# Causal attention and the feed-forward's input, moved tile by tile into the loop of the second cross attention

## The chip, the cores and the metric

The kernel runs on one core of one Trainium2 chip. The metric is the time of one execution on the device, in microseconds (us); of several runs the median is given. The core has five engines with instruction queues of their own: TensorE (PE: matrix products and transposes; its weight loads are shown as PEld), VectorE (DVE), ScalarE (ACT), GpSimd (POOL) and SyncE (SP, which here only issues DMAs). Each works through its own queue in program order and waits on semaphores.

## The reference

Two layers work on latents x of 16 x 64 rows by 256 columns, with a context of 16 x 1024 rows. All is 32-bit float, 16 heads of 16.

```
x = x + L0_cross(norm(x), ctx, mask)      x = x + L1_cross(norm(x), ctx)
x = x + L0_linear_attention(norm(x))      x = x + L1_attn(norm(x))
x = x + L0_ffn_int8(norm(x))              x = x + L1_ffn_fp4(norm(x))

L1_attn:  Q, K, V = per-head 16x16 maps of x;  a = softmax(causal(Q K' / 4));  out = a V
          cat = heads side by side (b, s, 256);  scrambled = cat.transpose(0,2,1).reshape(b, s, 256)
          return scrambled @ W_O
L1_ffn:   fp4(x): per block of 16 columns, scale = max|x|/6, round x/scale to a 4-bit grid, times scale
          h = silu(fp4(x) @ fp4(w_gate)') * (fp4(x) @ fp4(w_up)')       (704 columns)
          return fp4(h) @ fp4(w_down)'
```

The cross attention reads all 64 latents of a batch and all 1024 context rows. Causal attention works inside one batch, and the feed-forward on each row alone.

## The kernel before, in words

The latents lie in SBUF as `lat`, 8 tiles of 128 rows (two batches each). The program is a row of blocks; each block frees its semaphores and ends at a barrier of all engines. This text is about the last two, `second_cross` (L1_cross) and `last_tiles` (L1_attn and L1_ffn). PSUM is 8 banks of 128 x 512 floats.

`second_cross` runs 64 steps, 4 for each of 16 batches, two heads times two halves of the work in each. Step s of TensorE is: `scores(s)` into banks 0 to 3, in even steps `times_v` for an earlier pair of steps, `project_v(s+2)`, `transposes(s-1, 0)`, in steps whose batch s//4+1 isn't in `EarlyKeys.BATCHES` `project_k(s+4)`, then `transposes(s-1, 1)`; every eighth step (s = 10, 18, ...) ends with `output`, after which tile (s-10)/8 of `lat` is complete. `scores(s)` waits for both exponentials of step s-1. All results but the scores rotate through banks 4 to 7 (`Banks.open`), so an open waits until the result four opens earlier has been taken. VectorE takes the two maxima (L859), the values (L841), half of the transposed probabilities (L869) and, once both exponentials are done, the inverses of the two row sums in one instruction (`inverses`, L892). GpSimd multiplies the two probabilities of 128 x 1024 by them (`normalise`, L655). ScalarE computes the exponentials (L802) and takes keys (L772) and the other half of the transposed probabilities (L813). Among these steps the weights of the fp4 feed-forward are quantised (`Fp4Weights`): for each of three matrices x eight VectorE steps from step `FW_STEPS[x]` on, one a step, a GpSimd step, and three groups of transposes. The seventh of the eight, `scalar_tensor_tensor` of 128 x 1536, is L180. Lines 173 to 181 (`fp4_steps`) serve the weights, the feed-forward's input and its hidden layer.

After the 64 steps, three more drain the last two pairs. `last_tiles` then runs causal attention and the feed-forward over the 8 tiles in 12 rounds: in round r causal scores of tile r, the rest of causal attention of tile r-1, its output and the feed-forward's input of tile r-2, gate and up of tile r-3, the hidden layer's rounding, transposes and down projection of tile r-4. Its own norms take 4 tiles at once (`Norm`, `sn`) or one (`fn`). It has buffers of its own (two of `prob` and `hid`, three of `value`), and all 8 banks rotate.

Names and lines for the steps below. Causal, on TensorE: L1911 transposes of the normed latents, L1924 queries and keys, L1929 values, L1943 scores, L1955 transposes of the probabilities, L1971 heads, L1983 transposes back, L1994 output. On VectorE: L2075 and L2080 logits and maxima, L2086 and L2090 division, L2095 output. On GpSimd: L2057 `spread_queries`, L2064 `distances`. Feed-forward: L2126 transposes of its input, L2136 gate and up, L2147 transposes of the hidden layer, L2158 down; L2226 product with up on VectorE, L2176 SiLU and L2183 to L2187 hidden copies on ScalarE, L2258 the last scaling on GpSimd, L2262 output. Norms: L1839 to L1868, of which L1849 is the square root on ScalarE. SiLU, Exp and Sqrt each need their table loaded on ScalarE; a copy doesn't.

## Time and profile before

| | |
|---|---|
| time before, median of 3 runs | 1401.79 us (1398.05 to 1402.02) |
| the profiled execution: time, span | 1398.16 us, 1396.3 us |
| PE busy in the span | 1279.3 us (92%) |
| DVE, ACT, POOL busy | 930.5 (67%), 784.7 (56%), 689.2 us (49%) |
| scores of step 0 and of step 63 of `second_cross` start | 729.14 and 1167.27 us |
| first instruction of `last_tiles` | 1184.24 us |
| mean clock granted to TensorE | 0.969 of full |

The span runs from the first to the last instruction of the execution; the time is 1.9 us longer. Times are us from the span's start unless ns is said. A busy TensorE is not one at its peak, since its instructions overlap: where work is back to back, the start of the next group minus the start of this one is what a group costs. In the rows, "[0.59 <-DVE ca_v L841]" means 0.59 us of idle time in front of the row, ended by that instruction of VectorE.

### The profile page before, as it was taken

Reading aid. Unit: us, or ns where it says so; the run is one execution under the profiler, and the core shown is the slowest. Engines: PE = TensorE matmul, PEld = TensorE weight load, DVE = VectorE, ACT = ScalarE, POOL = GpSimd, SP = SyncE. Lnnn points to the kernel's source line nnn. Section 1 sums busy time; section 2 is a strip of 40 time slices with the busy share of each in tenths; the row PEclk is TensorE's granted clock in tenths of the full one; section 3 lists DMA queues with packets and bytes.
Section 4 is the critical chain, followed back from the end, with each engine's and each line's share of the span. In section 5 each row is a group of like instructions: output and inputs, shape, how many; then the busy total and the mean of one; then the engine's idle time right before and its main releaser. Section 6 shows DMA issues by size and latency. Waiting matters only on the chain. (4 is left out here: it accounts for less than half of the span.)

```text
span 1396.3 us, 28298 instructions
## 1 busy us (share of the span) xinstructions
PE 1279.3 (92%) x11120; PEld 890.4 (64%) x11122; DVE 930.5 (67%) x1728; ACT 784.7 (56%) x1350; POOL 689.2 (49%) x383
## 2 busy tenths in 40 slices
PE   6999999999999999887879999999999997778876
PEld 3667666676676675555546677667667765655653
DVE  4685686765665654765857686777677766568774
ACT  3766656666666654554646666665666564344431
POOL 2755655566665652320036574665557665323311
PEclk9999999999999999999999999999999999688998
DMA  4322112111123002004521021031022300000000
GB/s 159 93 70 66 48 46 67 46 47 47 58 81 103 13 16 99 1 1 135 170 66 62 31 62 52 31 92 52 32 61 63 92 1 13 16 2 5 9 8 12
DMA packets 30530, 74.21 MB, mean 53 GB/s; under 512 B 4032, under 2 KB 16192, under 8 KB 26176
## 3 DMA queue, kind: packets, MB, share of 16 engines
q1 hardware_dynamic: 30400, 72.41, 16.9%
q8 instruction: 90, 1.47, 0.4%
q14 instruction: 40, 0.33, 0.1%
HBM read 65.06 MB, written 7.34 MB: 52 GB/s over the span
## 5 line engine op out<-in xcount | busy, mean ns | idle before, releaser
L655 POOL TENSOR_TENSOR ca_prob<-ca_prob,ca_inv_sum 128x1024 f32<-128x1024 f32 x256 | 493.2, 1948 | 345.8 <-DVE ca_inv_sum L892 345.8
L732 PEld LDWEIGHTS bank<-ident,ca_prob 128*128 128x128 f32 x2048 | 236.6, 141 | 85.1 <-issue 57.8
L732 PE MATMUL bank<-ident,ca_prob 128*128 128x128 f32 x2048 | 265.3, 274 | 13.7 <-POOL ca_prob L655 7.8
L856 DVE CUSTOM_DVE_ANT_0 ca_neg_logit<-bank,ca_mask_add 128x1024 f32<-128x1024 f32 x128 | 151.6, 1221 | 112.5 <-PE bank L722 81.4
L859 DVE TENSOR_REDUCE ca_neg_max<-bank 128x1 f32<-128x1024 f32 x128 | 150.6, 1218 | 79.1 <-PE bank L722 79.1
L802 ACT ACTIVATE ca_prob<-bank,ca_neg_max 128x1024 f32<-128x1024 f32 x128 | 142.7, 1115 | 88.5 <-DVE ca_neg_max L859 88.5
L802 ACT ACTIVATE ca_prob<-ca_neg_logit,ca_neg_max 128x1024 f32<-128x1024 f32 x128 | 146.8, 1149 | 72.8 <-DVE ca_neg_max L856 72.7
L869 DVE COPY ca_probT<-bank 128x512 f32<-128x512 f32 x256 | 163.5, 680 | 2.1 <-PE bank L732 2.1
L813 ACT ACTIVATE ca_probT<-bank 128x512 f32<-128x512 f32 x256 | 139.1, 595 | 24.8 <-PE bank L732 22.1
L722 PE MATMUL bank<-ca_kT,ca_q_blk 32*128 32x512 f32 x1024 | 146.0, 639 | 4.6 <-DVE ca_v L841 2.7
L772 ACT ACTIVATE ca_kT<-bank,ca_bk 64x512 f32<-64x512 f32 x128 | 87.4, 683 | 104.4 <-PE bank L667 103.5
L749 PEld LDWEIGHTS bank<-ca_probT,ca_v 128*32 128x32 f32 x4096 | 109.0, 110 | 48.1 <-issue 31.2
L667 PE MATMUL bank<-ca_ctxT,ca_wk 128*128 128x512 f32 x256 | 122.5, 603 | 11.7 <-DMA ca_bk<-in_L_xattn_bk 9.2
L749 PE MATMUL bank<-ca_probT,ca_v 128*32 128x128 f32 x4096 | 126.3, 276 | 1.4 <-ACT ca_probT L813 1.4
L681 PE MATMUL bank<-wv,ctxT 128*128 128x256 f32 x512 | 127.2, 392 | 0.0
L681 PE MATMUL bank<-ca_wv,ca_ctxT 128*128 128x256 f32 x512 | 127.2, 392 | 0.0
L681 PEld LDWEIGHTS bank<-wv,ctxT 128*128 128x128 f32 x512 | 92.2, 189 | 41.2 <-issue 31.3
L681 PEld LDWEIGHTS bank<-ca_wv,ca_ctxT 128*128 128x128 f32 x512 | 92.2, 189 | 41.2 <-issue 28.2
L772 ACT ACTIVATE ca_kT<-bank,ek_bk 64x512 f32<-64x512 f32 x80 | 54.6, 683 | 66.2 <-PE bank L667 65.6
L667 PE MATMUL bank<-ctxT,ek_wk 128*128 128x512 f32 x160 | 74.9, 593 | 2.1 <-PEq L100 2.1
L667 PEld LDWEIGHTS bank<-ca_ctxT,ca_wk 128*128 128x128 f32 x256 | 44.7, 194 | 45.8 <-issue 35.7
L841 DVE TENSOR_TENSOR ca_v<-bank,bv 128x512 f32<-128x512 f32 x64 | 43.8, 685 | 26.4 <-PE bank L681 26.4
(278 smaller groups left out, 1648.4 us busy)
## 6 DMA issues: line engine op xcount, KB each, us to landing
ca_ctxT<-in_ctxT SPq DMA_DIRECT2D x16, 1024.0 KB, 5.2
ctxT<-in_ctxT SPq DMA_DIRECT2D x16, 1024.0 KB, 4.9
ca_mask_i<-in_mask SPq DMA_DIRECT2D x32, 256.0 KB, 4.5
ek_ctxT<-in_ctxT SPq DMA_DIRECT2D x12, 512.0 KB, 5.5
early_k<-ek_out SPq DMA_DIRECT2D x48, 128.0 KB, 3.5
ca_kT<-early_k SPq DMA_DIRECT2D x12, 512.0 KB, 5.7
lat<-in_x SPq DMA_DIRECT2D x1, 1024.0 KB, 4.8
out<-lat SPq DMA_DIRECT2D x8, 128.0 KB, 1.9
```

The source lines that it names most:

```text
L655: pool.tensor_tensor(self.prob[:, x, :], self.prob[:, x, :], self.inv_sum[:, x:x + 1].broadcast_to([P, CTX]), ALU.mult).then_inc(self.norm ...
L667: mm = pe.matmul(self.core.bank[:, x, :], self.wk[:, k, m * P:(m + 1) * P], self.ctxT[:, b % 2, k, half * HALF_CTX:(half + 1) * HALF_CTX], ...
L681: mm = pe.matmul(self.core.bank[:, x, r * D:(r + 1) * D], self.ctxT[:, b % 2, k, ch * P:(ch + 1) * P], self.wv[:, k, :], start=(k == 0), s ...
L722: mm = pe.matmul(self.core.bank[:, 2 * j + half, :], self.q_blk[rows, b % 2, u, :, :], self.kT[rows, b % 2, u, :], start=True, stop=True, ...
L732: tr = pe.transpose(self.core.bank[:, x, n * P:(n + 1) * P], self.prob[:, 2 * (s % 2) + p, (4 * h + n) * P:(4 * h + n + 1) * P], self.core ...
L749: mm = pe.matmul(self.core.bank[32 * j:32 * j + 32, x, 0:P], self.v[:, b % 2, ch, m * P + 32 * j:m * P + 32 * j + 32], self.probT[:, n % 2 ...
L772: op = act.activation(self.kT[half * S:(half + 1) * S, b % 2, 2 * m + r, :], self.core.bank[r * S:(r + 1) * S, x, :], ACT.Identity, bias=s ...
L802: act.activation(self.prob[:, y, :], source, ACT.Exp, bias=self.neg_max[:, y:y + 1], scale=-1.0 if self.masked else 1.0, accum_out=self.ro ...
L813: self.banks.free(act.activation(self.probT[:, n % 2, 4 * h:4 * h + 4, 2 * (s % 2) + p, :], self.core.bank[:, x, :].rearrange("p (n q) -> ...
L856: dve.tensor_tensor_reduce(self.neg_logit[:, p, :], scores, self.mask_add[:, b % 2, :], -1.0, BIG, ALU.add, ALU.min, self.neg_max[:, y:y + ...
L859: dve.tensor_reduce(self.neg_max[:, y:y + 1], scores, AX.X, ALU.max, negate=True).then_inc(self.max_ready, 1)
L869: self.banks.free(dve.tensor_copy(self.probT[:, n % 2, 4 * h:4 * h + 4, 2 * (s % 2) + p, :], self.core.bank[:, x, :].rearrange("p (n q) -> ...
```

## The change

The two blocks become one, `second_layer`. Causal attention of tiles 0 to 5, most of tile 6, and the quantised input of feed-forward tiles 0 to 4 go into the 64 steps, at fixed distances behind step 10+8t in which tile t of the cross attention is complete. `tile_at(s, lag)` gives the tile t with s = 10 + lag + 8t. Both norms take one tile at a time (`TileNorm`), with five VectorE steps behind the root instead of six. The steps' drain, causal attention's end (tiles 6 and 7) and all 8 feed-forward tiles come in an order written out by hand, with no barrier and no norm of 4 tiles between. `inverses` becomes two instructions, one for each probability, the first right behind the maxima; `normalise` waits for each alone. The eight VectorE steps of each weight matrix move to steps `FW_AT`. The feed-forward's division of its input moves from GpSimd to VectorE; the last rounding step of the hidden layer moves from VectorE to GpSimd. Causal attention's buffers lie in the memory of `EarlyKeys`, one of each instead of two or three; three hidden buffers lie in the weights' scratch. The causal weights load at the start of the block.

```diff
-        pool.wait_ge(self.inv_ready, s + 1)
         for p in range(2):
             x = 2 * (s % 2) + p
+            pool.wait_ge(self.inv_ready, 2 * s + p + 1)
...
-    def inverses(self, dve, s):
+    def inverse(self, dve, s, p):
+        y = 2 * (s % 2) + p
+        dve.wait_ge(self.exp_done, 2 * s + p + 1)
         if s >= 2:
+            dve.wait_ge(self.norm_ready, 2 * (s - 2) + p + 1)
+        dve.reciprocal(self.inv_sum[:, y:y + 1], self.row_sum[:, y:y + 1]).then_inc(self.inv_ready, 1)
...
-FW_STEPS = (4, 20, 36)
+FW_AT = ((2, 3, 4, 5, 6, 7, 8, 9), (17, 19, 21, 22, 25, 27, 29, 30), (37, 38, 41, 43, 45, 46, 49, 51))
+FW_SCALE = (10, 31, 52)
+FW_TRANSPOSE = ((12, 13, 14), (33, 34, 35), (54, 55, 56))
+def tile_at(s, lag):
+    n = s - 10 - lag
+    return [n // 8] if n >= 0 and n % 8 == 0 else []
... TensorE, step s of 64
                 ca.scores(pe, s)
                 if s % 2 == 0 and s >= 4:
                     ca.times_v(pe, s // 2 - 2)
                 if s + 2 < STEPS:
                     ca.project_v(pe, s + 2)
+                for t in tile_at(s, 3):
+                    sa.latent_transposes(pe, t, norm1.xn_ready)
+                for t in tile_at(s, 8):
+                    sa.heads(pe, t)
+                for t in tile_at(s, 16):
+                    ff.latent_transposes(pe, t)
                     ca.transposes(pe, s - 1, 0)
+                for t in tile_at(s, 5):
+                    sa.scores(pe, t)
+                for t in tile_at(s, 9):
+                    sa.back(pe, t)
+                for t in tile_at(s, 10):
+                    sa.output(pe, t)
                     ca.project_k(pe, s + 4)
                     ca.transposes(pe, s - 1, 1)
...
+                for t in tile_at(s, 3):
+                    sa.project(pe, t)
+                for t in tile_at(s, 7):
+                    sa.transposes(pe, t)
... ScalarE, at the end of a step
+                for t in tile_at(s, 1):
+                    norm1.root_on_scalar(act, t)
...
+                for t in tile_at(s, 12):
+                    norm2.root_on_scalar(act, t)
... VectorE, step s of 64
                 ca.maxima(dve, s)
+                ca.inverse(dve, s, 0)
                     ca.take_pv(dve, s // 2 - 2)
                     ca.take_v(dve, s + 2)
                     ca.take_t_on_vector(dve, s - 1, 0)
+                ca.inverse(dve, s, 1)
+                for t in tile_at(s, 2):
+                    causal_input(t)
+                for t in tile_at(s, 5):
+                    sa.logits(dve, t)
+                for t in tile_at(s, 9):
+                    sa.divide(dve, t)
+                for t in tile_at(s, 10):
+                    leave_causal(t)
+                for t in tile_at(s, 14):
+                    feed_forward_input(t)
+                for t in tile_at(s, 15):
+                    ff.round_x(dve, t)
... GpSimd, behind the two multiplications of a step
+                for t in tile_at(s, 4):
+                    sa.spread_queries(pool, t)
+                for t in tile_at(s, 6):
+                    sa.distances(pool, t)
... TensorE behind the steps
+            ff.project(pe, 0, 0)
+            ca.times_v(pe, 30)
+            ff.project(pe, 0, 1)
+            pe.wait_ge(ca.exp_done, 2 * STEPS)
+            banks.rotating = range(8)
+            for p in range(2):
+                ca.transposes(pe, STEPS - 1, p)
+            ff.project(pe, 1, 0)
+            ca.times_v(pe, 31)
...
+            gate_and_up(7)
+            for t in (5, 6, 7):
+                ff.hidden_transposes(pe, t)
+                ff.down(pe, t)
... VectorE behind the steps
+            ca.take_pv(dve, 30)
+            feed_forward_input(5)
+            ff.hidden(dve, 0)
+            ff.round_x(dve, 5)
+            ca.take_t_on_vector(dve, STEPS - 1, 0)
+            ff.round_hidden(dve, 0)
+            ca.take_pv(dve, 31)
+            ff.hidden(dve, 1)
+            leave_cross(7)
+            ff.round_hidden(dve, 1)
+            causal_input(7)
+            ff.hidden(dve, 2)
...
```

On VectorE `causal_input` is the five steps of `TileNorm.finish_on_vector`, `feed_forward_input` these five and four of `fp4_steps`, `round_x` the other four and a multiplication, `leave_cross` and `leave_causal` an output addition and three steps of statistics; `hidden` is two products and three of `fp4_steps`. GpSimd behind the steps runs, among the hidden layers' steps in tile order, `distances` of tiles 6 and 7 and, between the hidden tiles 1 and 2, `spread_queries(7)`.

## Rows read from the trace of the kernel before

**Rows 1.** The page: the TensorE clock granted, in 40 slices of 34.9 us.

```profile
PEclk9999999999999999999999999999999999688998
```

**Rows 2.** Busy time by stretch; columns us, engines' busy us (instructions), clock, DMA share, GB/s.

```profile
730.00:1167.30 437.30, 431.05 (x4128) 306.06 (x4124) 315.76 (x469) 269.52 (x469) 274.85 (x143) 1.00 0.17 50
1167.30:1184.20 16.90, 10.36 (x173) 7.79 (x172) 6.84 (x14) 5.30 (x10) 7.49 (x4) 1.00 0.01 1
1184.20:1396.30 212.10, 160.64 (x1392) 120.62 (x1392) 137.82 (x300) 79.27 (x141) 60.89 (x42) 0.83 0.03 10
```

**Rows 3.** Timeline of two steps with a key projection; columns start us, us, instruction.

```profile
903.69 1.14 PE L722 MATMUL bank<-ca_kT,ca_q_blk 32*128 32x512 f32 x8
...
904.76 1.99 PE L681 MATMUL bank<-wv,ctxT 128*128 128x256 f32 x8
904.90 2.35 DVE L859 TENSOR_REDUCE ca_neg_max<-bank 128x1 f32<-128x1024 f32 x2 [1.68 <-PE bank L722]
...
907.46 1.88 PE L667 MATMUL bank<-ctxT,ek_wk 128*128 128x512 f32 x4
...
909.20 4.38 POOL L655 TENSOR_TENSOR ca_prob<-ca_prob,ca_inv_sum 128x1024 f32<-128x1024 f32 x2 [2.38 <-DVE ca_inv_sum L892]
...
910.15 1.14 PE L722 MATMUL bank<-ca_kT,ca_q_blk 32*128 32x512 f32 x8
...
911.22 1.96 PE L749 MATMUL bank<-ca_probT,ca_v 128*32 128x128 f32 x64
```

**Rows 4.** Timeline, steps 10 and 11: late VectorE work and the bank that TensorE waits for.

```profile
803.51 2.72 DVE L180 SCALAR_TENSOR_TENSOR ca_fw_raw<-ca_fw_raw,ca_fw_e 128x1536 f32<-128x1536 f32 x1
...
809.24 1.16 PE L732 MATMUL bank<-ident,ca_prob 128*128 128x128 f32 x8 [0.59 <-DVE ca_v L841]
```

**Rows 5.** Timeline, a step without a key projection.

```profile
1161.21 1.09 PE L732 MATMUL bank<-ident,ca_prob 128*128 128x128 f32 x8 [0.33 <-POOL ca_prob L655]
```

**Rows 6.** The chain in order of time; columns start us, us, engine, tile, line.

```profile
1212.09 0.79 PE bank L1971 x52
...
1213.65 0.63 PE bank L1983 x4
...
1215.15 1.93 PE bank L1943 x32
1217.09 1.93 PE bank L1994 x16
1219.02 1.02 PE bank L1955 x8
1220.04 0.89 PE bank L1924 x8
1220.94 0.46 PE bank L1929 x4
```

**Rows 7.** The same chain: first and last of fourteen VectorE steps on one tile's input.

```profile
1222.36 0.18 DVE lt_fn_rstd L1857
...
1228.51 0.43 DVE lt_ff_x L2219
```

**Rows 8.** Timeline of POOL and VectorE in the last stage.

```profile
1202.30 1.89 POOL L2057 TENSOR_TENSOR lt_sa_q<-lt_sa_qk,small 128x1024 f32<-128x1024 f32 x1
...
1202.40 1.82 DVE L1861 TENSOR_TENSOR lt_sn_fix<-lt_sn_fix,lt_sn_var 128x4 f32<-128x4 f32 x1
```

**Rows 9.** Timeline of ScalarE: a table load and the root behind it.

```profile
1339.74 1.28 ACT L1849 ACT_TABLE_LOAD   x1
...
1341.03 0.20 ACT L1849 ACTIVATE lt_fn_std<-lt_fn_var 128x1 f32<-128x1 f32 x1
```

**Rows 10.** The chain (first row) and the timeline at the kernel's end.

```profile
1370.30 4.95 PE bank L2136 x16
...
1376.97 3.02 PE L2158 MATMUL bank<-fw_downT,lt_ff_hidT 128*128 128x256 f32 x12 [0.89 <-ACT lt_ff_hidT L2183]
...
1387.12 5.66 PE L2158 MATMUL bank<-fw_downT,lt_ff_hidT 128*128 128x256 f32 x12 [0.68 <-ACT lt_ff_hidT L2183]
```

More of the change, by code:

```diff
@@ new lines, in _ @@
+            ff.project(pe, 2, 0)
+            sa.transposes(pe, 6)
+            ff.project(pe, 2, 1)
+            ff.hidden_transposes(pe, 0)
+            sa.latent_transposes(pe, 7, norm1.xn_ready)
+            sa.heads(pe, 6)
+            ff.down(pe, 0)
+            sa.project(pe, 7)
+            ff.project(pe, 3, 0)
+            sa.back(pe, 6)
+            sa.scores(pe, 7)
+            ff.hidden_transposes(pe, 1)
+            ff.project(pe, 3, 1)
+            sa.output(pe, 6)
+            ff.down(pe, 1)
@@ new lines, in _ @@
+            ff.latent_transposes(pe, 5)
+            sa.transposes(pe, 7)
+            ff.project(pe, 4, 0)
+            sa.heads(pe, 7)
+            ff.hidden_transposes(pe, 2)
+            ff.project(pe, 4, 1)
+            sa.back(pe, 7)
+            ff.down(pe, 2)
+            sa.output(pe, 7)
+            gate_and_up(5)
+            ff.latent_transposes(pe, 6)
+            ff.hidden_transposes(pe, 3)
+            ff.down(pe, 3)
+            gate_and_up(6)
+            ff.latent_transposes(pe, 7)
```

1023 lines of the change are left out of this document (496 added, 527 removed).

## The prediction

> **What bounds the kernel now.** I read the clock row of the page first: granted full speed until the last stage, and well below it there [rows 1]. Then the busy times by stretch: in the 64 steps TensorE is busy for 431.1 of 437.3 us at clock 1.00, VectorE for 315.8, ScalarE 269.5, GpSimd 274.9; in the last stage TensorE is busy for 160.6 of 212.1 us at clock 0.83 [rows 2]. A busy TensorE may hide gaps, so I went to a timeline. Scores start at 903.69 and again at 910.15, which is 6.46 us, and between them stand values 904.76, transposes, keys 907.46, transposes 909.18, each starting before the one ahead has ended [rows 3]: TensorE bounds these steps. Starts give the costs: scores 1.07, values 1.83, keys 1.72, eight transposes 0.87 to 0.97; `times_v` about 1.88. A step with keys takes 6.46 (odd) or 8.34 us (even), and 4.74 or 6.62 is TensorE's work in one without. There it waits a little for `normalise`, 0.33 us in front of a transpose [rows 5]. The second bound of a step is the chain scores, maxima (start 1.2 behind the scores), two exponentials, next scores: 1.2 + 2.35 + 1.3 + 0.1, about 4.95 us [rows 3]. The last stage is bound by neither one engine nor the clock alone, but by waits of one tile's parts for each other.
>
> **What is removed.** Everything from the start of the last scores, 1167.27, to the span's end, 1396.3: 229.0 us. The new end is built up from zero below.
>
> **Added to the steps: TensorE.** One causal tile, from the chain where the clock was full [rows 6]: heads 0.79, back 0.45 (four transposes at 0.11; the row's 0.63 has the last one's latency), scores 1.93, output 1.93, probabilities' transposes 1.02, queries and keys 0.89, values 0.46, and the latents' two transposes 0.22: 7.7 us. Six tiles 46.2, tile 6's input and projections 1.6, five transposed feed-forward inputs 1.2: 49 us. In steps that TensorE bounds all of this lands on the path. In the twelve odd steps without keys some 0.4 us each was slack: minus 5. The old schedule put L180 at the end of steps 10, 26 and 42, behind a wait for that step's `output`; it ran to 806.2, the maxima started 2 us late, the values' bank came free late, and TensorE lost about 0.8 us [rows 4]. `FW_AT` moves it away: minus 3 with what follows. Sum so far +41.
>
> **Added to the steps: lateness.** VectorE now ends many steps later than the next scores. What it is late by isn't lost at once, but the values' bank is wanted again four opens later, as in [rows 4]. I walked through one period of eight steps for each kind of step.
> (a) The first `inverse` waits for an exponential that ends 0.25 us behind the maxima, and costs 0.17: values are taken 0.43 us later in every step, some 4.6 us behind the scores' start. `sa.scores` opens two banks behind the first transposes, at 1.07 + 1.83 + 0.87 = 3.8; the second is the values' bank: 0.8 us. Alike 0.6 in the steps with `project`, 0.4 with `back`, 0.5 where `sa.transposes` needs the keys' bank: 2.3 a period, 15 us in all.
> (b) `finish`, scaling and rounding of one input are fourteen VectorE steps, 1222.36 to 1228.94 in the old kernel [rows 7]; one stall of 1.5 and a division of 0.7 between them come off, the scaling that GpSimd did comes on with 0.43: 4.8 us of plain work. VectorE's two-input instructions in SBUF wait for a running GpSimd instruction: a one-column one took 1.82 us instead of 0.17 while GpSimd's second 1.89 ran [rows 8]. `normalise`'s second half starts 0.2 us behind the second inverse, just where the appended work begins, and in the step of `feed_forward_input` `distances` stands behind it: two stalls, 2.5 + 3.4 = 5.9 us; `round_x` one, 3.9. In steps with keys the next maxima are 3.4 us late, TensorE loses 2.5, then 1.3 to 2.2 in the step after: about 4.1 for each of tiles 0, 1, 2 and 4; for tile 3, in steps 48 to 50 without keys and with L180 on top, 8.9. Together 25 us.
> (c) `causal_input` (2.9) with `leave_causal` (1.4) in steps without keys, and step 29 with queries, L180 and projections: 9 us.
> (d) Each root takes two table loads of 1.28 and 0.2 [rows 9], 2.76 us at ScalarE's end of a step; the next exponential comes 1.5 late, the first `inverse` with it, the values' bank too. Six roots of the second norm fall in front of `sa.scores`: 9; the others 2, under `output`'s 1.93.
> That is 60 us. They overlap: a step in which TensorE waits gives VectorE and ScalarE time to catch up, so I take two thirds, 40, with ends 15 (only (a)) and 65. As a check, VectorE's 315.8 plus some 130 (new work, stalls, (a)) is 446 of a stretch of 437 + 41 + 40 = 518: high, but not the bound.
>
> The ports, waits and queues moved past: five causal weight loads on SP stand ahead of context loads that wait for values anyway, and are wanted 10 steps later; GpSimd's `spread_queries` and `distances` add 1.9 each to a step where it had 2 to 4 us idle. I cost both at nothing; were that cover gone, it is 1.9 us a time, six times.
>
> **The new end.** TensorE's work from the last scores on: gate and up 4.95 [rows 10], hidden transposes 0.8, down 2.8, eight times 68; three inputs' transposes 0.7; cross 9.6; causal tile 6's rest 6.2, tile 7's 7.7: 92 us, of which 81 until gate and up of tile 7 have ended. In-order waits on that way, from the order written out: `times_v(31)` for VectorE's copy behind `feed_forward_input(5)`, `hidden(0)` and `round_x(5)`, 3.1; the normed tile 7, 1.4; `output(7)` for `divide(7)` behind `round_x(6)`, 3.6; the input of tile 7, 1.6; copies of the hidden layer, 3: 13. Behind the last gate and up the old kernel took from 1375.25 to 1393.3, 18.05; its down ran 5.66 us where the one before took 3.02 [rows 10], a half clock after an idle TensorE that now has tiles 5 and 6 to do: minus 2.6; one rounding step on GpSimd (1.39) for VectorE's 0.89: plus 0.5; no output addition in between: minus 0.4. 15.5, and 3.0 to the span's end for the store. 81 + 13 + 15.5 + 3 = 112.5 us; ends 104 (few waits) and 122 (GpSimd's single order, in which `spread_queries(7)` stands ahead of the division of tile 2, holds VectorE for all it can).
>
> **Sum.** -229.0 + 41 + 40 + 112.5 = -35.5. On the profiled execution: 1396.3 - 35.5 + 1.9 = 1362.7 us. That execution was 3.6 us below the median of the runs, about the spread of the three; I keep 1363. The terms' ends give 1363 - 25 - 8 = 1330 and 1363 + 25 + 10 = 1398.
>
> **The table switch by the Trainium skill.** A load took 1283 ns and the root started 0.01 us behind it [rows 9]. The Trainium skill, ScalarE: Activation LUTs, section What ACT_TABLE_LOAD costs, says that every switch to another set costs about 2.66 us, since a drain of 1380 ns comes with it; this trace doesn't agree. It speaks against this change, and is the fourth rival.
>
> **Rivals.**
> 1. TensorE stays the only bound: lateness costs 10 and the end 104, so 1363 - 30 - 8 = 1325. For it: TensorE's 431 of 437, and VectorE's share. Against: [rows 4] shows that 2 us of lateness is paid, and (b) is more.
> 2. The clock falls in the new end. If it is granted 0.83 as in the old last stage, 92 us of work take 19 more: 1382. Against: that stage was idle for a quarter of its time, the new end for some 15%.
> 3. Slower: VectorE leads. If each of the twelve two-input or fast instructions of a tile's norms and rounding meets a GpSimd one, 8 more than I count, times 1.8 is 14 us a tile; with five and a half tiles 79, of which all lands once VectorE is the bound: over 1430; it decides against the kernel from 38 us, four more stalls a tile. Against: GpSimd has two, at most four instructions a step.
> 4. ScalarE is stopped for twice the load at each switch: 2.76 us more a root, behind the exponentials of 13 steps; 33 us: 1396. Against: [rows 9].
> 5. Doing little: the waits of the old last stage come back in the written order (TensorE's 13 us become 45), 1395. For it: the last tiles still have their 15.5 us chain.
>
> **How the numbers follow.** Forecast 0.62; rival 1 0.15; rival 2 0.11; rival 3 0.07; rival 4 0.02; rival 5 0.03. 0.3% (4 us) is about what can be told from no change. Slower: rival 3, 0.07. Same: the top of the forecast and of 4 and 5, 0.04. Faster 0.89. The range reaches from 1330, which leaves out most of rival 1, to 1396.
>
> **What would show it.** Scores of step 63 start near 1248 (1167.3 + 41 + 40); TensorE's waits in the steps are for VectorE (values, and `picked`), largest in steps 25, 33, 41, 49 and 57; L180 stalls no bank; ScalarE has some 25 loads more in the steps; the clock is 1.0 until the last 20 us; from the last scores to the end 112 us. The prediction is wrong if the steps take under 495 us (rival 1) or over 545, or if the end takes over 125.

## The result and the profile after

The changed kernel takes 1420.65 us (median of 4 runs, 1411.11 to 1421.45); the kernel before, beside it, 1400.52. The ratio is 1.0136 with a 95% interval of 1.0116 to 1.0156: slower by 1.4%, where 1363 us was forecast. The quickest of the four runs, 1411.11 us, was granted a mean clock of 0.975, the other three 0.965 to 0.966, so some us of the distances between medians below are such differences of the clock. The profiled execution took 1421.31 us, its span is 1418.0 us. The page gives the granted clock in 40 slices, here of 35.4 us, in tenths of full speed:

```profile
PEclk9999999999999999999999999999899989999999
```

The low stretch at the end that [rows 1] shows is gone, but the mean over the span is 0.965, where it was 0.969. The loss has moved. Busy time by stretch, from the first scores to those of step 63 and from there to the end (columns as in [rows 2]):

```profile
724.58:1291.18 566.60, 513.41 (x4980) 369.48 (x4980) 423.74 (x712) 328.61 (x561) 294.13 (x156) 0.95 0.13 39
1291.18:1418.00 126.82, 103.87 (x713) 73.73 (x712) 77.72 (x155) 43.46 (x82) 49.74 (x32) 0.91 0.03 9
```

Cut alike, the kernel before has 438.1 us (TensorE busy for 431.9, clock 1.00) and 229.0 us (171.0, clock 0.84). So the end gave back 102.2 us, and the steps took 128.5. Of these, 81.5 are more busy time of TensorE and 47 are idle time: 53.2 us now against 6.2. Who ended the idle time, in the view of waits for TensorE in the steps of the changed kernel (us in total, times, longest):

```profile
PE bank L732 <- DVE ca_v L841: 24.4, 12, 5.1
PE bank L1792 <- DVE ca_v L841: 7.6, 3, 2.8
PE bank L1792 <- POOL ek_ctxT L1908: 5.7, 3, 3.0
PE bank L1843 <- DVE ca_attnT L883: 5.3, 6, 0.9
```

L732 are the transposes of the probabilities, whose second bank is that of the values (L841), as in [rows 4]. The two rows of L1792 are new: causal scores, six times, wait for the same values or for GpSimd's `spread_queries` (L1908). All waits for the values, the row for L667 and one of L722 with them, are 35.8 of 54.3 us.

One gap shows most of the causes at once. Timeline of the changed kernel, steps 23 and 24 (scores of 23 at 901.91, of 24 at 916.69; 14.78 us, the longest distance of all):

```profile
900.65 3.33 POOL L655 TENSOR_TENSOR ca_prob<-ca_prob,ca_inv_sum 128x1024 f32<-128x1024 f32 x1 [1.25 <-DVE ca_inv_sum L892]
...
903.71 1.28 ACT L1706 ACT_TABLE_LOAD   x1
903.95 1.04 POOL L638 TENSOR_TENSOR ca_q_blk<-ca_q,small 128x512 f32<-128x512 f32 x1
...
904.94 1.89 POOL L1908 TENSOR_TENSOR ek_ctxT<-ek_ctxT,small 128x1024 f32<-128x1024 f32 x1
905.00 0.20 ACT L1706 ACTIVATE ca_fn_std<-ca_fn_var 128x1 f32<-128x1 f32 x1
905.22 1.28 ACT L802 ACT_TABLE_LOAD   x1
906.52 1.11 ACT L802 ACTIVATE ca_prob<-bank,ca_neg_max 128x1024 f32<-128x1024 f32 x1
...
907.75 0.16 DVE L892 RECIPROCAL ca_inv_sum<-ca_row_sum 128x1 f32<-128x1 f32 x1 [2.28 <-ACT ca_prob L802]
907.84 0.69 DVE L841 TENSOR_TENSOR ca_v<-bank,bv 128x512 f32<-128x512 f32 x1
...
908.67 2.68 PE L1792 MATMUL bank<-ek_ctxT 64*128 64x64 f32 x32 [2.83 <-DVE ca_v L841]
...
911.28 3.78 PE L667 MATMUL bank<-ctxT,ek_wk 128*128 128x512 f32 x4
```

Read it from the bottom. The keys (L667) take 3.78 us, where they take 1.88 at the full clock [rows 3]: this is the lower of TensorE's two levels. It sets in during the causal scores ahead of them (2.68 for 2.00), right behind a gap of 2.83 us. The gap ends with the values (907.84), which VectorE takes behind the first `inverse` (907.75); that one waits 2.28 us for an exponential that starts at 906.52, behind two table loads and the root. And until 906.83 TensorE would have waited anyway: `spread_queries` of this tile is the last thing in GpSimd's step 22, behind its two `normalise` and `queries`, and ends only then. That part, 1.0 of the 2.83 us, stays whatever becomes of the loads and the values. A switch costs 1.28 us and the root starts 0.01 us behind it, as in [rows 9]. The Trainium skill, ScalarE: Activation LUTs, section What ACT_TABLE_LOAD costs, has 2.66 us for a switch; this trace doesn't agree either, so what was the fourth rival is not the cause.

The step of the feed-forward's input, tile 0 (same view):

```profile
923.79 1.90 POOL L655 TENSOR_TENSOR ca_prob<-ca_prob,ca_inv_sum 128x1024 f32<-128x1024 f32 x1 [1.25 <-DVE ca_inv_sum L892]
923.80 1.90 DVE L1712 SCALAR_TENSOR_TENSOR ca_fn_fix<-ca_fn_rstd,ca_fn_var 128x1 f32<-128x1 f32 x1
...
925.04 1.14 PE L722 MATMUL bank<-ca_kT,ca_q_blk 32*128 32x512 f32 x8
...
925.64 1.90 POOL L1915 TENSOR_TENSOR ek_out<-ek_out,ca_sa_top 128x1024 f32<-128x1024 f32 x1
...
925.92 1.64 DVE L1717 TENSOR_TENSOR ca_fn_rstd<-ca_fn_rstd,ca_fn_fix 128x1 f32<-128x1 f32 x1
...
929.45 2.36 DVE L859 TENSOR_REDUCE ca_neg_max<-bank 128x1 f32<-128x1024 f32 x2
...
932.87 1.36 PE L732 MATMUL bank<-ident,ca_prob 128*128 128x128 f32 x8 [2.17 <-DVE ca_v L841]
...
936.50 2.09 PE L722 MATMUL bank<-ca_kT,ca_q_blk 32*128 32x512 f32 x8
```

Two one-column instructions take 1.90 and 1.64 us, the first beside the second half of `normalise`, the second beside `distances` (L1915). The maxima start 4.41 us behind the scores instead of 1.2, and TensorE waits 2.17, where term (b) has 2.5. Behind it the scores take 2.09 us where 1.14 is the full clock; this the sum did not have.

The end, TensorE alone: step 63 and the stretch where the order is written out:

```profile
1295.71 3.68 PE L1792 MATMUL bank<-ek_ctxT 64*128 64x64 f32 x32 [2.37 <-POOL ek_ctxT L1908]
...
1316.84 3.64 PE L749 MATMUL bank<-ca_probT,ca_v 128*32 128x128 f32 x64 [4.04 <-issue]
1320.42 3.81 PE L1993 MATMUL bank<-fw_upT,xnT 128*128 128x352 f32 x8
...
1333.85 0.44 PE L1761 MATMUL bank<-ident,ek_ctxT 128*128 128x128 f32 x2 [2.50 <-DVE ek_ctxT L1719]
...
1366.32 2.99 PE L1843 MATMUL bank<-ek_ctxT 64*64 64x256 f32 x16 [3.11 <-DVE ek_ctxT L1943]
...
1387.54 0.61 PE L1983 MATMUL bank<-ident,ca_ff_x 128*128 128x128 f32 x2 [2.92 <-DVE ca_ff_x L2069]
...
1390.11 5.19 PE L2015 MATMUL bank<-fw_downT,wi_downT 128*128 128x256 f32 x12 [0.69 <-ACT wi_downT L2038]
```

All but the first of the long waits are at the places forecast. The profile names no releaser for the 4.04 ("issue"); what ended it is in the experiment on the end's order. With smaller ones TensorE is idle for 16.5 us until the last gate and up have ended, where 13 was forecast, and for 23.0 in the whole end. Behind three of them it runs at the lower clock: causal scores 3.68 for 2.00, `times_v` 3.64 for 1.96 and up 3.81 for 2.53, down 5.19 for 3.02.

### The profile page after: what moved, and what is told of

Read it like the earlier page. It is cut to its first block and busy times, and to the rows that moved or that the text cites. A ratio compares the mean times of both kernels' runs of the same rounds, so it can differ in the third digit from the quotient of the medians.

```text
span 1418.0 us, 28592 instructions
## 1 busy us (share of the span) xinstructions
PE 1294.1 (91%) x11120; PEld 899.6 (63%) x11122; DVE 976.0 (69%) x1876; ACT 802.0 (57%) x1373; POOL 690.7 (49%) x383
## 5 line engine op out<-in xcount | busy, mean ns | idle before, releaser
L732 PEld LDWEIGHTS bank<-ident,ca_prob 128*128 128x128 f32 x2048 | 240.9, 143 | 102.5 <-issue 75.2
L732 PE MATMUL bank<-ident,ca_prob 128*128 128x128 f32 x2048 | 273.7, 278 | 29.2 <-DVE ca_v L841 25.4
L722 PE MATMUL bank<-ca_kT,ca_q_blk 32*128 32x512 f32 x1024 | 150.3, 657 | 4.5 <-DVE ca_v L841 2.7
L749 PE MATMUL bank<-ca_probT,ca_v 128*32 128x128 f32 x4096 | 129.5, 280 | 4.9 <-issue 4.0
L667 PE MATMUL bank<-ca_ctxT,ca_wk 128*128 128x512 f32 x256 | 121.8, 601 | 10.1 <-DMA ca_bk<-in_L_xattn_bk 9.1
L667 PE MATMUL bank<-ctxT,ek_wk 128*128 128x512 f32 x160 | 79.5, 624 | 4.4 <-DVE ca_v L841 2.4
L667 PEld LDWEIGHTS bank<-ca_ctxT,ca_wk 128*128 128x128 f32 x256 | 44.6, 193 | 43.6 <-issue 33.3
L892 DVE RECIPROCAL ca_inv_sum<-ca_row_sum 128x1 f32<-128x1 f32 x256 | 40.6, 159 | 41.6 <-ACT ca_prob L802 34.4
```

Of the source, the lines that this page charges most:

```text
L667: mm = pe.matmul(self.core.bank[:, x, :], self.wk[:, k, m * P:(m + 1) * P], self.ctxT[:, b % 2, k, half * HALF_CTX:(half + 1) * HALF_CTX], ...
L722: mm = pe.matmul(self.core.bank[:, 2 * j + half, :], self.q_blk[rows, b % 2, u, :, :], self.kT[rows, b % 2, u, :], start=True, stop=True, ...
L732: tr = pe.transpose(self.core.bank[:, x, n * P:(n + 1) * P], self.prob[:, 2 * (s % 2) + p, (4 * h + n) * P:(4 * h + n + 1) * P], self.core ...
L749: mm = pe.matmul(self.core.bank[32 * j:32 * j + 32, x, 0:P], self.v[:, b % 2, ch, m * P + 32 * j:m * P + 32 * j + 32], self.probT[:, n % 2 ...
```

## Experiments

Each kernel was compared with the kernel before beside it (medians of 1398.3 to 1400.6). Steps and end are cut as above and taken from the profiled execution; "waits" is the sum of TensorE's waits in the steps. Differences in the text are between medians. Steps, waits, clock and end are those of one execution, which lay up to some 5 us from its kernel's median, to either side (no_table_loads 4.9 below, pool_first_alone 5.2 above). Steps in which nothing was changed differ by 4 to 5 us between the profiled executions of some pairs (both_edits and both_tail), so less than that is not read from this column.

| kernel | us | ratio (interval) | steps | waits | clock in the steps | end |
|---|---|---|---|---|---|---|
| before | 1400.5 | 1 | 438.1 | 7.4 | 1.00 | 229.0 |
| changed | 1420.7 | 1.0136 (1.0116 to 1.0156) | 566.6 | 54.3 | 0.95 | 126.8 |
| before_split | 1396.2 | 0.9974 (0.9963 to 0.9986) | 438.7 | 6.8 | 1.00 | 228.3 |
| values_first | 1406.2 | 1.0045 (1.0027 to 1.0063) | 551.5 | 43.8 | 0.96 | 127.7 |
| pointer_norm | 1396.0 | 0.9973 (0.9959 to 0.9986) | 547.6 | 46.4 | 0.97 | 123.0 |
| no_table_loads | 1395.2 | 0.9959 (0.9948 to 0.9971) | 543.0 | 44.4 | 0.97 | 123.1 |
| no_input_rounding | 1412.3 | 1.0091 (1.0073 to 1.011) | 553.9 | 48.8 | 0.96 | 127.7 |
| dummy_matmuls | 1410.4 | 1.0079 (1.0064 to 1.0094) | 558.2 | 49.5 | 0.97 | 125.2 |
| pool_first_alone | 1405.2 | 1.0039 (1.0022 to 1.0056) | 558.4 | 47.6 | 0.95 | 124.5 |
| spread_first_alone | 1412.2 | 1.0094 (1.006 to 1.0127) | 563.1 | 53.3 | 0.95 | 123.3 |
| both_edits | 1390.4 | 0.994 (0.9918 to 0.9963) | 543.7 | 39.0 | 0.96 | 123.4 |
| both_no_loads | 1384.7 | 0.9908 (0.9889 to 0.9928) | 535.5 | 38.4 | 0.98 | 121.5 |
| both_tail | 1384.3 | 0.9892 (0.9878 to 0.9907) | 539.3 | 39.0 | 0.97 | 119.9 |
| tail_and_dummy | 1389.2 | 0.994 (0.992 to 0.996) | 544.4 | 39.3 | 0.98 | 123.2 |
| pool_first | 1364.7 | 0.9754 (0.9735 to 0.9773) | 521.3 | 26.7 | 0.98 | 117.6 |
| pool_first_and_dummy | 1371.2 | 0.9804 (0.9785 to 0.9824) | 527.5 | 25.1 | 0.98 | 115.9 |
| pool_first_no_loads | 1358.5 | 0.9705 (0.9691 to 0.972) | 518.8 | 25.7 | 0.99 | 113.4 |
| pool_first_l180 | 1367.0 | 0.9764 (0.9742 to 0.9786) | 521.8 | 27.7 | 0.99 | 119.4 |

### The split alone

The kernel before, with two inverses instead of one, in both cross attentions:

```diff
                 ca.maxima(dve, s)
+                ca.inverse(dve, s, 0)
...
-                ca.inverses(dve, s)
+                ca.inverse(dve, s, 1)
```

> The kernel before, with only the inverses split in two, the first right behind the maxima, in both cross attentions. Theory: alone the split costs little, since nothing there makes the first exponential late: within 4 us of before (values 0.4 us later against normalise 1.3 us earlier). Rival (the split itself is what makes the steps long): 15 us slower or more.

The steps of the second cross attention are as long as before (438.7 for 438.1) and the whole is 3.5 us shorter than the kernel before beside it (1399.7); in the profiled executions the scores of step 0 start 6.2 us earlier, so what it gave lies ahead of these steps, where the first cross attention has the split too. Where VectorE has little else to do the early inverse costs nothing on the path. The rival, that the split itself makes the steps long, is out; whether term (a), 15 us, is a cost beside the other work, the next run tells.

### Values ahead of the first inverse

```diff
                 ca.maxima(dve, s)
-                ca.inverse(dve, s, 0)
                 if s % 2 == 0 and s >= 4:
                     ca.take_pv(dve, s // 2 - 2)
                 if s + 2 < STEPS:
                     ca.take_v(dve, s + 2)
+                ca.inverse(dve, s, 0)
```

> The changed kernel, with one edit: on VectorE the first inverse of a step stands behind the picked values and take_v instead of right behind the maxima. Theory: TensorE's idle time in the steps (47 us more than before, nearly all until VectorE has taken values) comes through the values' bank, and each idle gap is followed by half clock (about 28 us). With this edit take_v no longer waits for the first exponential, 0.4 us earlier in every step and 2.3 us earlier where two table loads delay it; the three waits of 2.8, 2.8 and 2.0 us in front of the causal scores should go, and the half clock behind them: 10 to 20 us less than the changed kernel. Rival (VectorE is late at the start of the step because of the appended work, whatever the order): under 5 us less.

14.4 us less than the changed kernel. TensorE's waits fall by only 10.5, and they change their name: the causal scores' 7.6 for values and 5.7 for `spread_queries` become one row for GpSimd.

```profile
PE bank L732 <- DVE ca_v L841: 21.7, 11, 5.1
PE bank L1792 <- POOL ek_ctxT L1908: 11.4, 5, 3.7
```

(Waits of values_first, steps.) The values had hidden that GpSimd's `spread_queries` was late as well: with the values early, TensorE waits at the same place for it, and nearly as long. The gain isn't term (a) alone either: in the gap of steps 23 and 24 the first inverse, and the values behind it, were held by the table loads of term (d), and this order takes the values out of that wait too.

### The norm's one-column instructions

```diff
-        dve.scalar_tensor_tensor(self.fix[:, :], self.rstd[:, :], self.rstd[:, 0:1], self.var[:, :], ALU.mult, ALU.mult)
+        dve.tensor_scalar(self.fix[:, :], self.rstd[:, :], self.rstd[:, 0:1], self.var[:, 0:1], ALU.mult, ALU.mult)
...
-        dve.tensor_tensor(self.rstd[:, :], self.rstd[:, :], self.fix[:, :], ALU.mult)
+        dve.tensor_scalar(self.rstd[:, :], self.rstd[:, :], self.fix[:, 0:1], None, ALU.mult)
```

> The changed kernel, with the two steps of a tile's norm that read two SBUF tensors (one column each) written as tensor_scalar with pointer scalars; the same values. Theory: these two waited for GpSimd's running multiplication (1.89 and 1.64 us instead of 0.17), twelve times the first and five times the second in the steps, about 28 us of VectorE's time at places where it is late; without them TensorE's gaps of 2.2 to 5.1 us behind feed_forward_input shrink by some 3 us each and the half clock with them: 15 to 30 us less than the changed kernel. Rival (the one-column tensor_scalar with two pointers waits as well): no change.

24.7 us less, by an edit of two lines that computes the same. VectorE's groups (mean ns behind the comma), of the changed kernel:

```profile
L1712 DVE SCALAR_TENSOR_TENSOR ca_fn_fix<-ca_fn_rstd,ca_fn_var 128x1 f32<-128x1 f32 x5 | 9.5, 1893 | 0.2
L1717 DVE TENSOR_TENSOR ca_fn_rstd<-ca_fn_rstd,ca_fn_fix 128x1 f32<-128x1 f32 x5 | 8.2, 1637 | 0.2
L1719 DVE TENSOR_SCALAR ca_ff_x<-lat,ca_fn_mv,ca_fn_rstd 128x256 f32<-128x256 f32 x5 | 2.1, 414 | 0.2
```

and of pointer_norm (six times, since this view reaches one tile further):

```profile
L1719 DVE TENSOR_SCALAR ca_ff_x<-lat,ca_fn_mv,ca_fn_rstd 128x256 f32<-128x256 f32 x6 | 6.8, 1135 | 0.2
L1712 DVE TENSOR_SCALAR ca_fn_fix<-ca_fn_rstd,ca_fn_var 128x1 f32<-128x1 f32 x6 | 1.6, 272 | 0.2
L1717 DVE TENSOR_SCALAR ca_fn_rstd<-ca_fn_rstd,ca_fn_fix 128x1 f32<-128x1 f32 x6 | 1.3, 214 | 0.2
```

The one-column form with its operands as scalars is not held up; the stall moves on to the first wide instruction (L1719), and of two a norm about one is left. With no GpSimd instruction beside them the two one-column instructions of the changed kernel took 220 and 159 ns, so the scalar form costs 50 ns more there. The Trainium skill, SBUF — State Buffer, section Who interferes with whom, says that a VectorE instruction with two SBUF inputs contends with a GpSimd one that reads SBUF, and that `tensor_scalar` does so in its two-port modes; the first half agrees with L1712 and L1717 of the changed kernel (1893 and 1637 ns), the second with L1719 (1135 ns for 414), though no row tells whether L1719 ran in such a mode.

### The table loads

The norms' root replaced by a copy on ScalarE, which needs no table; the normed values differ, and nothing else is changed:

```diff
-        act.activation(self.std[:, :], self.var[:, :], ACT.Sqrt)
+        act.activation(self.std[:, :], self.var[:, :], ACT.Copy)
```

> The changed kernel with the root left out: ScalarE copies the variance instead of taking its square root, so no table is loaded for it and the normed values differ. Theory: thirteen pairs of loads of 1.28 us in the steps delay the next exponential and with it the first inverse and the values' bank; without them 8 to 20 us less than the changed kernel (five or six gaps of some 2 us in front of the causal scores and the half clock behind each). Rival (ScalarE has idle time enough): no change.

25.4 us less, above the 8 to 20 expected. Taken by itself this would make the loads the main cause. So the three were put together, first values_first with pointer_norm, then the loads out as well:

> The changed kernel with both edits of values_first and pointer_norm; the same values. Theory: the two act on different gaps (those in front of the causal scores, those behind feed_forward_input), so their gains of 14 and 25 us add up to some 35: 1383 to 1389, 10 us or more below before. Rival (both only give VectorE back time that one of them already gives): 1394 to 1396, no better than pointer_norm.

> both_edits with the root left out (ScalarE copies instead, so no table loads in the norms and other values). Theory: with the values' bank freed ahead of the first inverse, the loads delay the exponentials alone, which TensorE's work covers in most steps: 5 to 12 us less than both_edits, and not the 25 that the same edit gave the changed kernel. Rival (the loads cost on their own): 20 us less or more. What is still above the work of 41 us then is the end's and the plain lateness.

14.4 and 24.7 give 30.2 together, not 39, and 1390.4 lies just outside the 1383 to 1389 expected; and the loads, 25.4 alone, are worth 5.7 on top. The gains are not terms of a sum: each edit takes away the part of a gap by which its cause ended last.

### Matmuls that nobody needs

Three 512-column matmuls into a bank that causal scores open next, in the causal scores of tiles 1, 3 and 5:

```diff
-        x = [self.banks.open(pe, ("ss", t, g)) for g in range(2)]
+        x = [self.banks.open(pe, ("ss", t, 0))]
+        if t in (1, 3, 5):
+            for n in range(3):
+                pe.matmul(self.core.bank[:, x[0], :], self.core.ident[:, :], self.core.xnT[:, 0, 0:512],
+                          start=True, stop=True)
+        x.append(self.banks.open(pe, ("ss", t, 1)))
```

> The changed kernel with three more matmuls of 512 columns (2.6 us of TensorE's time, results overwritten) where it waits 2.0 to 2.8 us for the values' bank, ahead of the causal scores of tiles 1, 3 and 5. Theory (the clock falls because TensorE is idle there, and that costs as much again as the wait): the causal scores and keys behind them run at full clock (keys 1.9 us, not 3.8, in step 23), and the kernel is 3 to 10 us faster than the changed one, though TensorE does 7.7 us more. Rival (the wait alone costs, the clock falls for another reason): no change, or up to 3 us slower.

10.3 us faster by the medians, 8 by the two ratios, whose intervals don't meet, with 7.8 us more for TensorE to do. The gap of steps 23 and 24 in this kernel (L1788 the unneeded ones, L1797 the causal scores):

```profile
906.71 2.84 PE L1788 MATMUL bank<-xnT,ident 128*128 128x512 f32 x6 [1.04 <-POOL ek_ctxT L1913]
...
909.48 2.00 PE L1797 MATMUL bank<-ek_ctxT 64*128 64x64 f32 x32
911.41 1.98 PE L667 MATMUL bank<-ctxT,ek_wk 128*128 128x512 f32 x4
```

The causal scores start 1.0 us later behind their step's scores than without (7.75 for 6.76), but they and the keys run at the full clock: 2.00 for 2.68 and 1.98 for 3.78. So the half clock behind a gap is a cost of its own, and filling the gap takes it away. The Trainium skill, TensorE: Matmul & The Clock Gate, section A second HAM failure mode: psum-queue depth-cycling, tells of a kernel whose short idles between groups, as it cycled through the banks, made the clock swing; the granted 0.95 of a stretch with 53 us of such idles agrees.

It doesn't work for every gap. On the fastest kernel of that stage (both_tail, below):

> Edit: the fastest kernel so far (1384.3) and the same three unneeded 512-column matmuls ahead of the second bank of causal scores of tiles 1, 3 and 5 that made the changed kernel 10.3 us faster. In this kernel the wait behind them is shorter (1.5 to 2.6 us where it was 2.4 to 2.8) and the clock is 0.97 in the steps instead of 0.95. Theory (they fill a gap and keep the clock, worth less where the gaps are fewer): 2 to 7 us less, 1377 to 1382. Rival (what they filled is gone, their 7.7 us of work lands on the path): 2 to 8 us more.

5.0 us slower. There the gap that is left ends with `spread_queries`, and TensorE waits for it ahead of the unneeded matmuls: they start at 905.13 behind a wait of 2.13, where the causal scores of both_tail start at 904.96 behind the same wait. At that place all of their 2.8 us land on the path. Where there is hardly a gap (pool_first, below, has 0.48 us in step 23):

> Edit: pool_first with the three unneeded matmuls. Where the causal scores' wait for spread_queries is gone there is no gap left to fill. Theory: 2 to 7 us slower than pool_first, since 7.7 us of work now lands on the path; if it is faster, the matmuls act through the clock and not through the gap they stand in. Rival: the same gain as in tail_and_dummy, 2 to 7 us less than pool_first.

6.5 us slower than pool_first, for 7.8 us of work.

### The input's rounding left out

```diff
     def divide_x(self, dve, t, xn_ready):
+        if t < 5:
+            dve.wait_ge(xn_ready, t + 1)
+            return
...
     def round_x(self, dve, t):
+        if t < 5:
+            dve.memset(self.xinv[:, 0:1], 1.0).then_inc(self.x_ready, 1)
+            return
```

> Edit: the changed kernel, with the fp4 quantisation of the feed-forward's input left out for tiles 0 to 4 (VectorE's eight rounding steps a tile, 3.3 us of plain work each, and the GpSimd stall behind the first of them); the norm stays, and the input goes to the products unrounded. Values differ. It prices the VectorE part of term (b). Theory (five sources of lateness share the same steps, each gap costs its idle time and a half clock): 12 to 22 us less than the changed kernel, 1399 to 1409, and the maxima of steps 25, 33 and 41 come within 9.5 us of the ones before. Rival A (only the root's loads and the norm's stalls make the gaps, the rounding hides in VectorE's slack): 0 to 6 less. Rival B (VectorE is the bound, each us of its work lands whole): the 5 times 5 us of plain work and stall, and their clock, 25 to 33 less.

8.4 us less, between the theory and rival A. L732's wait for values falls from 24.4 to 17.4 us; the maxima of the step behind tile 0's input come 10.13 us behind the ones before instead of 11.55. Of the rounding's 16.5 us of plain work and its stalls half or more is hidden. The run took 22.7 us of busy time from VectorE in the steps and gave 8.4 us; pointer_norm took 13.0 and gave 24.7. L732's wait for values fell about alike, to 17.4 and 15.7. So VectorE's busy time isn't what is paid, which speaks against rival B; that term (b) is for the greater part the norm's two stalls fits this, but isn't shown, since pointer_norm changes the norms of causal attention too.

### The end's order

On top of both_edits, VectorE's copy of the last transposed probabilities ahead of `hidden(0)` and `round_x(5)`:

```diff
             feed_forward_input(5)
+            ca.take_t_on_vector(dve, STEPS - 1, 0)
             ff.hidden(dve, 0)
             ff.round_x(dve, 5)
-            ca.take_t_on_vector(dve, STEPS - 1, 0)
```

> both_edits, and at the end VectorE copies the transposed probabilities of the last step ahead of the hidden layer of tile 0 and the rounding of tile 5's input. Theory: times_v(31) waited 4.0 us for that copy and ran at half clock behind it with the gate and up that follow: 4 to 9 us less than both_edits. Rival (the end is bound by the hidden layers' chain on VectorE and GpSimd): no change.

6.2 us less than both_edits. The end is 3.5 us shorter. The wait in front of `times_v(31)`, 4.15 us in both_edits, and the half clock behind it (3.22 for 1.96) are gone, so it was that copy that ended it; a wait of 2.01 us for `ca_attnT`, in front of the output (L759), has come a few us later. The other 2.7 are within what the unchanged steps vary by. At 1384.3 it is below the kernel before and the changed one. What it still waits for in the steps:

```profile
PE bank L732 <- DVE ca_v L841: 16.1, 11, 4.4
PE bank L1792 <- POOL ek_ctxT L1908: 11.4, 5, 3.7
```

### GpSimd's order

```diff
             for s in range(STEPS):
+                for t in tile_at(s, 4):
+                    sa.spread_queries(pool, t)
+                for t in tile_at(s, 6):
+                    sa.distances(pool, t)
                 ca.normalise(pool, s)
                 if s % GROUPS == 2 and s // GROUPS + 1 < B:
                     ca.queries(pool, s // GROUPS + 1)
-                for t in tile_at(s, 4):
-                    sa.spread_queries(pool, t)
-                for t in tile_at(s, 6):
-                    sa.distances(pool, t)
```

> Edit: the fastest kernel so far (both edits in the steps and VectorE's copy first at the end, 1384.3), and GpSimd's spread_queries and distances stand ahead of that step's normalise instead of behind it. The waits of causal scores for spread_queries (1.5 to 3.7 us, six times in its trace) should go. Theory (those waits and the half clock behind them are paid): 4 to 9 us less, 1375 to 1380. Rival A (they overlap with waits for VectorE's values, which then come in their place): within 3 us of 1384. Rival B (normalise now starts late, because GpSimd is busy for 1.9 us when the first inverse comes, and the transposed probabilities are late): 2 to 8 us more.

19.6 us less than both_tail, more than any theory had: 1364.7 us, ratio 0.9754 (0.9735 to 0.9773), the fastest kernel that computes all of it. The waits of pool_first in the steps:

```profile
PE bank L732 <- DVE ca_v L841: 10.5, 10, 3.2
PE bank L1792 <- DVE ca_v L841: 4.7, 6, 2.1
```

The 11.4 us for GpSimd are gone, 4.7 of them come back as waits for values, and L732's wait fell by 5.6 as well: 12.3 us of waits in all, and 18.0 us of the steps. GpSimd is idle between its `normalise` of one step and the first inverse of the next; the two instructions now lie there. Whether this was so in the changed kernel too:

> Edit: the changed kernel with only GpSimd's spread_queries and distances ahead of that step's normalise. On top of the other edits this gave 19.6 us. Theory (it takes away 5.7 to 11 us of waits of causal scores and the half clock behind them, whatever the rest; in the changed kernel three of the six waits end with VectorE's values and stay): 8 to 18 us less than the changed kernel's 1420.7, so 1403 to 1413. Rival A (GpSimd's place is the main cause of the miss, all of it is paid in the changed kernel too): 18 to 25 less, 1396 to 1403. Rival B (in the changed kernel VectorE's late values cover it): under 5 less.

> Edit: the changed kernel with only spread_queries ahead of that step's normalise; distances stays behind it. Theory (the wait is for spread_queries): within 4 us of pool_first_alone. Rival (what counts is distances, which in the step of the feed-forward's input runs behind normalise and holds VectorE's rounding up by 1.9 us a tile): within 4 us of the changed kernel, or half of the gain at most.

15.4 us and 8.5 us less than the changed kernel. The first is in the theory's range. The second is about half of it, and not clear of noise: its interval, 1.0060 to 1.0127, reaches into that of the changed kernel. Its trace shows that `spread_queries` alone had little to give in the steps. The six waits of the causal scores are now all for the values and still 11.9 us, of 13.3 before; only the wait of 2.37 us in step 63 is gone whole. What `distances` adds is plain in the traces. Its 1.9 us behind `normalise` stand where VectorE's L1717 is held up (925.64 1.90 on GpSimd, 925.92 1.64 on VectorE). The same instruction with only `spread_queries` moved, and with both:

```profile
L1717 DVE TENSOR_TENSOR ca_fn_rstd<-ca_fn_rstd,ca_fn_fix 128x1 f32<-128x1 f32 x5 | 8.2, 1635 | 0.2
L1717 DVE TENSOR_TENSOR ca_fn_rstd<-ca_fn_rstd,ca_fn_fix 128x1 f32<-128x1 f32 x5 | 0.8, 159 | 0.2
```

With both moved the waits of L732 for values fall from 24.4 to 17.1 us, and those of 1.7 to 2.2 us in steps 25, 33, 41 and 57, each behind a feed-forward's input, are 0.7 us or less.

With the loads out of pool_first:

> Edit: pool_first (1364.7), with the norms' root replaced by a copy on ScalarE, so that no table is loaded for it; values differ. It tells what the table loads still cost where the other edits are in. The same edit gave 25.4 us on the changed kernel and 5.7 on both edits. Theory (loads now lie in slack): 3 to 9 us less, 1356 to 1362. Rival (with the GpSimd waits gone the loads are the next gap): 10 to 20 less.

6.2 us less, as the theory had it: where the other edits are in, the loads for the norms' roots cost about a quarter of what they seemed to cost in the changed kernel. In the profiled executions most of it lies in the end (117.6 to 113.4), not in the steps (521.3 to 518.8). And the weights' L180 in another step:

```diff
-FW_AT = (..., (37, 38, 41, 43, 45, 46, 49, 51))
+FW_AT = (..., (37, 38, 41, 43, 45, 46, 47, 51))
```

> Edit: pool_first (1364.7), with the third weight matrix's seventh step (L180, 1.62 us on VectorE) in step 47 instead of step 49, where round_x of tile 3 stands. TensorE's longest wait in the steps of pool_first, 3.25 us, starts before that instruction (it is from the feed-forward's input in step 48), but the maxima of step 50 start 1.6 us late behind it. Theory: 1 to 4 us less, 1361 to 1364. Rival (step 47 has the logits and step 48 the input, and VectorE's 1.62 us then add to the wait of 3.25): 1 to 4 us more.

2.3 us more by the medians, with intervals that overlap: no gain. The wait of 3.25 us in front of L732 became 3.48, and steps 48 to 51 take 33.7 us where they took 33.1. The lateness only changed its step.

## Why the prediction was wrong

**The sum.** From the forecast (1362.7 on the profiled execution) to 1421.3 it is 58.6 us. The steps took 47.5 more than the forecast 81, the end 14.3 more than 112.5, the first scores came 4.6 earlier, and 1.4 lie outside the span. Both of the prediction's own signs of being wrong came: the steps took 566.6 us (over 545) and the end 126.8 (over 125).

**The steps' work, 49 less credits of 8: the clock.** TensorE is busy for 81.5 us more, 32.5 over the 49. A clock of 0.95 over 566.6 us is worth up to 28.3 of these; the rest is 4 us. With clock 0.99 (pool_first_no_loads) TensorE is busy for 494.0, or 62.1 over before, 5.2 of them for the clock: 57 for the 49. So the work was counted 4 to 8 us too low. The step that failed by most is that the clock stood in the sum for the end alone (rival 2): for the steps it was taken as the 1.00 of [rows 2], though the same sum put 40 us of gaps into them. dummy_matmuls shows that the clock behind a gap is paid. Of the credits, steps 10 and 11, where L180 was, took 16.55 us and now take 15.67: 0.9 us, once.

**The lateness, 40.** Idle time rose by 46.9. Much of it was seen: the values' bank, in 35.8 of the 54.3 us of waits; step 49 as the worst, with 5.07; the stalls of 1.9 and 1.6; maxima 3.2 late for 3.4. The places were only in part those named: next to step 49 the longest waits are in steps 31 (3.00), 23 and 39 (2.83) and 53 (2.76); 25, 33 and 41 have 2.2 each, 57 has 1.7. Taking two thirds was too low by 7 us, and with the credits of 8, most of which were not seen, it makes 15. The whole list of 60 less these 8 is 52, or 5 too high. (a) 15, (d) 11 and (b) 25 can't be set one by one against the 14.4, 25.4 and 24.7 us of values_first, no_table_loads and pointer_norm: each of these edits takes away a part of gaps that other terms share, and the clock behind them. What the list lacked is that half clock.

**What was costed at nothing.** `spread_queries` and `distances` were said to lie in 2 to 4 us of GpSimd's idle time, and 1.9 us a time if that cover were gone. The cover was looked for in the length of the step, not in the order: both stand behind `normalise`, and the first, in all but the last of its steps, behind `queries` too. TensorE wants it one step later; in step 23 it ends at 906.83, and TensorE was ready at 905.84. The second holds up VectorE's L1717 in the step of the feed-forward's input; this second stall was in term (b), but not that GpSimd's order was its cause and could be had for nothing. The order is worth 15.4 us in the changed kernel, with waits of 54.3 us falling to 47.6, and 19.6 once the other edits are in. Next to the clock it is the largest error, and the two overlap. The bound given, 11.4 us, is near the 12.3 us of waits that the order took away on top of the other edits, but 5.6 of these are L732's, which the bound did not mean.

**The end, 112.5.** 126.8 measured. Until the last gate and up have ended it took 109 us for 94. Idle time is 16.5 for 13: 4.04 (3.1 forecast) at `times_v(31)`, 2.50 (1.4), 3.11 (3.6), 2.92 (1.6), and one not counted, 2.37 for `spread_queries`. Busy time is 92.5 for 81, and the clock of 0.89 over this stretch is worth up to 12.0, which is the whole of it: this is rival 2, at less than its 19 us. The rest took 14.5 us to the last addition (15.5 forecast), at full clock. With GpSimd's order changed the end took 117.6 at 0.95, and 113.4 at 0.97.

**The rivals.** The second came true in the end, at 12 us, and in the steps too, where neither the sum nor any rival had it. The third had the sign and the wrong mechanism: VectorE was busy for 423.7 of 566.6 us in the steps and was no bound; its lateness was paid gap by gap. The fifth didn't happen: the end gave back 102 us. The fourth falls by the 0.01 us between load and root; by its own numbers it would have been 36 us (13 times 2.76), not 33. That 1364.7 us of pool_first lies so near to the 1363 forecast means little: it has four edits that the forecast kernel doesn't have. It doesn't make the forecast of this one right.

What stays open: how the cost splits between the loads, the stalls and GpSimd's order in the changed kernel. The edits of the values' place, the stalls, the loads and GpSimd's order give 14.4, 24.7, 25.4 and 15.4 singly, which is 80; together with the end's 6.2 they gave 62. Only differences between neighbouring kernels were measured, and they depend on what else is in. Also open is what decides whether and when the clock falls behind a gap; a part of each single gain may be that.

## What to carry over

When work is put into a loop that TensorE fills, write for each moved instruction what stands ahead of it in its own queue at that moment and who wants it next; idle time in a step is no cover if the instruction can only start behind the one that ends the step. Price each gap of a full TensorE at more than its length: in the kernels of the table that took away 5 us of waits or more, each microsecond of them took 1.2 to 2.4 us of the steps with it (1.3 to 2.0 where 15 us or more went, which stands further out of the noise); the lower clock of the matmuls behind is the part that the traces show. And where several causes end a gap within a microsecond or two, one experiment at a time misleads in both directions, so stack the edits before ranking them.

## What the runs showed of the hardware

- More matmuls made the kernel faster: three groups of 2.6 us in front of a wait gave 10.3 us. In the same place they cost 5.0 us where they stood behind the wait, and 6.5 us where there was hardly a wait.
- The lower clock followed a gap of 2.83 us (keys 3.78 us behind it), but not one of 2.13 us in both_tail (keys 1.98), and in pool_first keys took 3.35 us behind a gap of only 0.26. The one gap in front doesn't tell it, nor how soon: in step 39, behind the same wait of 2.83 us, causal scores and keys took 2.00 and 3.66 us in the changed kernel, 3.68 and 3.17 in pointer_norm.
- A one-column VectorE instruction with pointer scalars took 272 and 214 ns where the same product with tensor operands took 1893 and 1637 ns beside a running GpSimd instruction, and 220 and 159 without one. A `tensor_scalar` of 128x256 (L1719) is held up as the others are: 0.41 us alone, up to 1.88 in pool_first.
- A load of ScalarE's table took 1.28 us, and the root started 0.01 us behind it.
